# A second pair of weight buffers, the weight split spread over a head, and four small VectorE operations with two tensor operands

## The reference

```python
x = layernorm(x)
qkv = silu(causal_conv4(x @ Wqkv))          # q, k, v of 16 heads
z, beta = x @ Wz, sigmoid(x @ Wb)
g = -exp(A_log) * softplus(x @ Wa + dt_bias)
q, k = l2norm(q) / sqrt(128), l2norm(k)
for t in range(512):                        # per head, M is 128 x 128
    M = M * exp(g[t])
    M = M + outer(k[t], (v[t] - k[t] @ M) * beta[t])
    out[t] = q[t] @ M
out = rmsnorm(out) * norm_w * silu(z)
x = x_in + layernorm(out @ Wout)
```

## Time and profile before

| | us |
|---|---|
| median of 3 runs (2894.02 to 2895.68) | 2894.31 |
| the profiled execution | 2893.81 |
| its span, first to last instruction | 2891.9 |
| PE busy | 2690.6 (93%) |
| DVE busy | 2257.9 (78%) |
| ACT busy | 2143.2 (74%) |
| POOL busy | 1892.7 (65%) |

### The profile page before, as it was taken

The page is one execution under the profiler, slowest core; times in us unless marked ns, Lnnn a source line. Parts: engine busy times, 40 slices in busy tenths (PEclk is TensorE's granted clock), DMA queues, the critical chain, the costliest instruction groups (busy, mean ns, idle before and its releaser), DMA issues. The chain is left out here.

```text
span 2891.9 us, 70042 instructions
## 1 busy us (share of the span) xinstructions
PE 2690.6 (93%) x23604; PEld 2278.7 (79%) x23604; DVE 2257.9 (78%) x5006; ACT 2143.2 (74%) x7286; POOL 1892.7 (65%) x1706
## 2 busy tenths in 40 slices
PE   3399999999999999999999999999999999986998
PEld 2288888888888888888888888888888888873554
DVE  5588888888888888888888888888888888853433
ACT  2388888888888888788888887888888887861211
POOL 2267777777777777777777777777777777751000
PEclk9699999999999999999999999999999999997999
DMA  5322222222222222222222222222222222201100
GB/s 190 126 87 94 89 87 77 95 89 83 82 87 96 89 81 82 96 89 80 83 96 89 87 77 95 89 83 82 87 96 89 81 82 89 89 5 53 36 29 29
DMA packets 78567, 241.78 MB, mean 84 GB/s; under 512 B 8336, under 2 KB 21520, under 8 KB 61584
## 3 DMA queue, kind: packets, MB, share of 16 engines
q1 hardware_dynamic: 78224, 237.41, 23.3%
HBM read 223.75 MB, written 13.63 MB: 82 GB/s over the span
## 5 line engine op out<-in xcount | busy, mean ns | idle before, releaser
L744 DVE SCALAR_TENSOR_TENSOR conv<-pj,cw,conv 128x511 f32<-128x511 f32 (+2 forms) x1152 | 847.0, 744 | 54.6 <-ACT conv L619 40.5
L926 PE MATMUL pj<-xt,w_hi 128*128 128x512 f32 x2048 | 694.5, 421 | 23.1 <-DVE wo L738 23.1
L539 POOL TENSOR_TENSOR kq<-kq,cum 128x512 f32<-128x512 f32 x256 | 428.1, 1693 | 0.0
L926 PEld LDWEIGHTS pj<-xt,w_hi 128*128 128x128 f32 x2048 | 354.5, 193 | 70.2 <-DVE wo L738 23.5
L926 PE MATMUL pj<-xt,w_lo 128*128 128x512 f32 x1024 | 409.3, 400 | 0.0
L568 POOL TENSOR_TENSOR inv<-inv,x 128x512 f32<-128x512 f32 x128 | 148.1, 1157 | 379.0 <-ACT inv L678 379.0
L619 ACT ACTIVATE conv<-pj,cw 128x512 f32<-128x512 f32 x384 | 266.0, 693 | 143.6 <-PE pj L926 133.4
L818 DVE TENSOR_TENSOR y<-bk,mask 128x256 f16<-128x256 f32 x512 | 216.3, 422 | 167.8 <-PE bk L992 160.3
L575 POOL TENSOR_TENSOR attn<-attn,part 128x512 f32<-128x512 f32 x256 | 326.5, 1276 | 9.0 <-ACT part L701 9.0
L638 ACT ACTIVATE squares_out<-tr 128x128 bf16<-128x128 f32 x1024 | 273.0, 299 | 47.8 <-PE tr L933 47.8
L1072 PE MATMUL pj<-wo,yt 128*128 128x256 f32 x1024 | 282.6, 399 | 0.8 <-DVE yt L869 0.8
(11 more groups left out here) (159 smaller groups left out, 7559.3 us busy)
## 6 DMA issues: line engine op xcount, KB each, us to landing
xt<-xt_scratch SPq DMA_DIRECT2D x128, 1024.0 KB, 4.8
decay<-decay_scratch SPq DMA_DIRECT2D x128, 256.0 KB, 5.3
cum<-cumdecay_scratch SPq DMA_DIRECT2D x128, 256.0 KB, 5.5
w_raw<-in_w_heads SPq DMA_DIRECT2D x16, 512.0 KB, 3.4
xt_scratch<-xt_hi SPq DMA_DIRECT2D x8, 512.0 KB, 2.8
xt_scratch<-xt_lo SPq DMA_DIRECT2D x8, 512.0 KB, 3.8
res<-in_x SPq DMA_DIRECT2D x8, 512.0 KB, 4.8
out<-yo SPq DMA_DIRECT2D x8, 512.0 KB, 3.1
```

The lines of the kernel that those rows point to most:

```text
L539: last = nc.gpsimd.tensor_tensor(part, part, of(cum, p)[:, :], ALU.mult)
L744: nc.vector.scalar_tensor_tensor(out=conv[:, i, j:SEQ], in0=pj[:, i % 2, 0:SEQ - j], scalar=cw[:, i, p // NSEQ, TAPS - 1 - j:TAPS - j], in ...
L926: last = nc.tensor.matmul(pj[:, i % 2, :], w[:, kt, cols], x_[:, kt, :], start=(n == 0), stop=(n == 3 * KT - 1))
```

## The change

There are two w_hi and two w_lo, used by even and odd heads, and `project` takes those of its head. A split waits for the projections of the head before the one that is being worked on (`NSEQ * (head - 1)`), which used the same buffers. The splits for the next head are called at the end of the odd slots: Q in slot 1, K in 3, V in 5, Z in 7, each after `add(0)`. The four splits of the first head stay before the loop.

Four small DVE operations get another form. `norms`, `q_norm` and `state_scale` become `scalar_tensor_tensor` with two tensor operands in SBUF (the added operand of the first two is the input itself, with a max or min that returns the first result). `rhs(0)` becomes `scalar_tensor_tensor` that subtracts a new tensor of zeros, which POOL fills before its loop and for which DVE has one more wait. `state_scale` had two tensor operands before.

```diff
-    w_hi = buf(ctx, "w_hi", [P, KT, 4 * P], F32R)
-    w_lo = buf(ctx, "w_lo", [P, KT, 4 * P], F32R)
+    w_hi = [buf(ctx, f"w_hi{i}", [P, KT, 4 * P], F32R) for i in range(2)]
+    w_lo = [buf(ctx, f"w_lo{i}", [P, KT, 4 * P], F32R) for i in range(2)]
+    zeros = buf(ctx, "zeros", [P, P])
...
-            pool.wait_ge(filled, 2)
+            nc.gpsimd.memset(zeros[:, :], 0.0).then_inc(filled, 1)
+            pool.wait_ge(filled, 3)
...
+                    hi, lo = w_hi[head % 2][:, :, cols], w_lo[head % 2][:, :, cols]
                     pool.wait_ge(w_in, DMA * (head + 1))
-                    wait(pool, proj[i], NSEQ * head)
-                    nc.gpsimd.tensor_copy(w_hi[:, :, cols], w_raw[:, :, cols]).then_inc(w_copied[i], 1)
+                    wait(pool, proj[i], NSEQ * (head - 1))
+                    nc.gpsimd.tensor_copy(hi, w_raw[:, :, cols]).then_inc(w_copied[i], 1)
                     pool.wait_ge(w_copied[i], head + 1)
-                    nc.gpsimd.tensor_tensor(w_lo[:, :, cols], w_raw[:, :, cols], w_hi[:, :, cols].bitcast(F32),
-                                            ALU.subtract).then_inc(w_split, 1)
+                    nc.gpsimd.tensor_tensor(lo, w_raw[:, :, cols], hi.bitcast(F32), ALU.subtract).then_inc(w_split, 1)
...
                 scale_b(a - 1)
-                if slot == 0 and head:
-                    split(V, head)
                 unit_diagonal(a - 1)
                 scale_k_tok(a - 2)
                 out_norm(a - 4)
-                if slot == NSEQ - 1:
-                    split(Q, head + 1)
                 first_transpose(a - 1)
                 scale_kq(a - 1)
                 low_b(a - 1)
-                if slot == 0 and head:
-                    split(Z, head)
                 add(1, a - 4)
-                if slot == NSEQ - 1:
-                    split(K, head + 1)
                 k_norm(a - 1)
                 inverse(a - 2)
                 add(0, a - 4)
+                if slot % 2:
+                    split(slot // 2, head + 1)
...
-                    nc.vector.tensor_scalar(of(k2, p)[:, :, :], of(sums, p)[:, :, :], EPS, None, ALU.add).then_inc(k2_ready, 1)
+                    nc.vector.scalar_tensor_tensor(out=of(k2, p)[:, :, :], in0=of(sums, p)[:, :, :], scalar=EPS,
+                                                   in1=of(sums, p)[:, :, :], op0=ALU.add, op1=ALU.max).then_inc(k2_ready, 1)
...
-                    nc.vector.tensor_scalar(of(q2, p)[:, :], of(k2, p)[:, 1, :], EPS * P, None, ALU.mult).then_inc(q2_ready, 1)
+                    nc.vector.scalar_tensor_tensor(out=of(q2, p)[:, :], in0=of(k2, p)[:, 1, :], scalar=EPS * P,
+                                                   in1=of(k2, p)[:, 1, :], op0=ALU.mult, op1=ALU.min).then_inc(q2_ready, 1)
...
-                    nc.vector.tensor_tensor(of(f, p)[:, :], of(f, p)[:, :], beta[:, :, p], ALU.mult).then_inc(f_ready, 1)
+                    nc.vector.scalar_tensor_tensor(out=of(f, p)[:, :], in0=of(f, p)[:, :], scalar=1.0, in1=beta[:, :, p],
+                                                   op0=ALU.mult, op1=ALU.mult).then_inc(f_ready, 1)
...
                     if c == 0:
+                        dve.wait_ge(filled, 3)
                         wait(dve, v_tok_ready, p + 1)
                         wait(dve, kn_ready, p + 1)
-                        nc.vector.tensor_scalar(r[:, 0, :], of(v_tok, p)[:, 0, :], of(kn, p)[:, 0:1], None,
-                                                ALU.mult).then_inc(r_ready[0], 1)
+                        nc.vector.scalar_tensor_tensor(out=r[:, 0, :], in0=of(v_tok, p)[:, 0, :],
+                                                       scalar=of(kn, p)[:, 0:1], in1=zeros[:, :],
+                                                       op0=ALU.mult, op1=ALU.subtract).then_inc(r_ready[0], 1)
...
+                    hi, lo = of(w_hi, p // NSEQ), of(w_lo, p // NSEQ)
                     for kt in range(KT):
-                        for w, x_ in ((w_hi, x_hi), (w_hi, x_lo), (w_lo, x_hi)):
+                        for w, x_ in ((hi, x_hi), (hi, x_lo), (lo, x_hi)):
```

## The result

The changed kernel takes 2853.19 us (median of 4 runs, 2852.80 to 2854.09) against 2894.26 us for the one before (4 runs). The ratio is 0.9858, with a 95% interval of 0.9845 to 0.9871: 41 us faster. 2852 was forecast.

The account below looks back on a forecast made before the run. PE's stream was taken to set the 18.65 us period. From 2893.8 us, -67.5 for boundaries and +25 for splits gave 2851.3, with 0.5 for the median 2852 us; own range 2845 to 2860 (chance 0.60), wider range 2823 to 2868.

Parts of the forecast that it names:

- Boundary, -67.5 us: At 15 head boundaries, POOL's wait for PE and what follows cost 4.5 us each; the second buffers remove it all.
- The splits' price, 25 us: In 60 periods after a split, DVE and with it PE are late by 0.42 us: 25 us, bounds 0 and 30.
- PE's own wait on w_split is met 8 steps early: PE's wait for the split weights of the next head is satisfied 8 steps before it matters.
- f held until the subtraction ends, 0.43 us: DVE's state_scale (L781) meets the split's subtraction on POOL and ends with it, 0.43 us late; lower bound no delay.
- r's new form, +0.07: DVE's rhs(0) (L847), 128 elements, takes 0.35 instead of 0.28 us in its new form; bounds 0 and +0.07.
- Slack of 0.08 us ahead of rhs(1): DVE could start rhs(1) (L851) 0.08 us earlier but waits for PE's from_state_k(1); delay beyond that reaches PE.
- b_hi hidden: ACT's b_hi ends 0.42 us before PE's z_first asks for it; both move by the same, so it stays hidden.
- The hold of r and q by scale_b: DVE's q or r loses 0.85 us to POOL's scale_b in every period, worth nothing to PE.
- The rival with q behind the diagonal: In 60 periods q waits for POOL's unit_diagonal (L513), PE losing 0.56 us each: 34 us, total 2886; chance 0.13.
- That margin: After a held r, q was estimated to start 0.03 us before POOL's unit_diagonal.

Follow-up runs that it names:

- version without boundary waits and without collision: The changed kernel with each split moved ahead of POOL's inverse, where POOL idles waiting for ACT: 2829.74 us.
- write-only experiment: The changed kernel with the w_lo subtraction replaced by a POOL memset for all heads but the first (does not compute the layer): 2831.38 us.
- the two halves of the experiments: The changed kernel with the old DVE forms, only second buffers and spread splits: 2848.05 us, set against the changed kernel's 2853.19 us.
- added reciprocals: Three more DVE reciprocals behind q_norm in every step, against the kernel with splits ahead of POOL's inverse and old forms (2829.73 us): 2841.27 us.
- the order with r and q first: The changed kernel with rhs(0) and q_norm moved ahead of decay_b on DVE, splits left in place: 2837.40 us.
- The forms alone: The kernel before with the four DVE operations in their new forms and nothing else changed: 2893.04 us, ratio 0.9995.
- the idle-time kernels: The changed kernel with each split moved ahead of POOL's inverse: 2829.74 us with the new DVE forms, 2829.73 us with the old.

## Why the prediction was right

- Boundary, -67.5 us: the version without boundary waits and without collision is 64.5 us below the kernel before (2829.74 against 2894.26). In the trace before, the 15 boundary periods are 66.8 us over 18.65 and single other periods 0.9; in the version without boundaries single periods still add 3. Those I did not trace, and the prediction left no term for them.
- The splits' price, 25 us: 60 x 0.42 was 1 us too much, since only 58 splits fall into full periods. That 2852 was met within 1.2 us is in part luck, for this and the 3 us without a term are of opposite sign.
- "PE's own wait on w_split is met 8 steps early" is wrong, and nothing rested on it: the splits of Q, K, V and Z end 119, 84, 50 and 19 us before their first use, which is 6, 4, 2.6 and 1 periods.
- f held until the subtraction ends, 0.43 us: 0.42 measured, in 54 steps. The write-only experiment shows that it is the reading.
- r's new form, +0.07: 5 us between the two halves of the experiments, 0.34 against 0.28 us in the rows.
- Slack of 0.08 us ahead of rhs(1), and PE paying for the rest: long periods 19.07 and short ones 18.66, where 19.05 to 19.10 and 18.65 were named. The added reciprocals put the slack at 0.10.
- b_hi hidden at the changed kernel: yes; the order with r and q first shows that little was left.
- The hold of r and q by scale_b is worth nothing to PE: shown by the order with r and q first, whose steps without a split have no hold and take 18.67 us. The forms alone and the idle-time kernels do not show it, since the hold is there in all of them.
- The rival with q behind the diagonal did not come: q took 0.15 us after a held r, L515 starting 0.08 us after it. That margin was estimated at 0.03.

What the prediction did not ask is whether the new place of the splits is worth having. Once there are two pairs of buffers it is worse than the old one: 2848 with the spread, 2840 without it, both with the old forms.

## What to carry to other kernels

An operation moved into an engine's idle time also moves onto what that engine shares: look what the neighbour runs in the same half microsecond, and whether both read SBUF. Slack is a number for one place, not for an engine: DVE idle 2.4 us of 18.65 had 0.1 us where PE waited for it. Two changes made together should be priced apart: here the second pair of buffers brought 54 us alone, and the new places of the splits and the new forms took 13 of them back. When a wait is taken off a chain, price the next thing on the same chain before claiming the whole wait.

## What the runs showed of the hardware

A DVE operation of only four elements with two SBUF inputs stood 0.42 us behind a POOL subtraction, and one of 128 elements stood behind a CAST, which has one input (0.53 us, 0.32 when it met nothing). Neither was held by a POOL memset of 0.74 us. `scalar_tensor_tensor`, `tensor_tensor` and `tensor_scalar` on SBUF were all held. It goes the other way too: a POOL operation that started 0.24 us behind DVE's scan of two SBUF inputs took 2.09 us instead of 1.16. Which of two operations that start some 0.02 us apart gets through is not stable: r was held in 18 of 128 periods with the forms alone and in 89 of the changed kernel, with the same time for the short periods in both.
